# Attention with eight routed experts: sorting the tokens of six half batches by expert, and computing keys and queries half a batch at a time

## The reference

```
latent = (x@Wk + x@Wv) @ W_down_kv;  k = latent@W_up_k;  v = latent@W_up_v;  q = x@Wq
scores = clip(q.k * scale) * exp(-0.0001*|i-j|);  attn = softmax(scores)
x = layernorm(x + (attn@v) @ Wo)
logits = x@w_router; top 2 of 8 experts, softmax of their two logits = weights
moe = sum over the 2 chosen e of weight * (silu(x@fc1[e][:, :128]) * (x@fc1[e][:, 128:])) @ fc2[e]
shared = (silu(x@gate_w) * (x@up_w)) @ down_w          # width 256
x = layernorm(x + moe + shared)
```

## Time and profile before

| | us |
|---|---|
| median of 3 runs | 810.48 (803.38 to 810.81) |
| the profiled execution | 815.1 |
| its span, first to last instruction | 813.1 |
| TensorE, ScalarE, VectorE, GpSimd busy | 763.2, 563.2, 367.1, 222.7 |

### The profile page before, as it was taken

How to read it: one execution, slowest core, us unless ns; L and a number is a source line. 1 busy time by engine, 2 the same in 40 slices (tenths; PEclk the granted TensorE clock), 3 DMA queues, 4 the chain that set the end, 5 groups by cost and what they waited for, 6 DMA issues and landing times. The chain is left out here.

```text
span 813.1 us, 14409 instructions
## 1 busy us (share of the span) xinstructions
PE 763.2 (94%) x4889; PEld 344.9 (42%) x4889; DVE 367.1 (45%) x974; ACT 563.2 (69%) x686; POOL 222.7 (27%) x168
## 2 busy tenths in 40 slices
PE   6736999999999999999999999999999999999996
PEld 4422333333333333333333333334666665665664
DVE  1733233232333233333233333333777777777774
ACT  4635799997999999999999999996222222222221
POOL 1619478392000000000000000000534534534533
PEclk9876699997999999999999999999999999999999
DMA  6489939688323324224233242700000000000000
GB/s 178 160 287 233 318 101 323 233 257 276 86 52 85 70 52 101 54 56 99 52 77 77 52 91 64 174 1 15 1 2 25 27 0 26 26 0 26 13 7 20
DMA packets 27797, 77.17 MB, mean 95 GB/s; under 512 B 2496, under 2 KB 18304, under 8 KB 20608
## 3 DMA queue, kind: packets, MB, share of 16 engines
q1 hardware_dynamic: 24320, 51.74, 25.8%
q0 software_dynamic: 3456, 25.17, 8.5%
HBM read 41.24 MB, written 35.65 MB: 95 GB/s over the span
## 5 line engine op out<-in xcount | busy, mean ns | idle before, releaser
L520 ACT ACTIVATE probs<-ps 128x1024 f32<-128x1024 f32 x480 | 446.8, 1063 | 32.4 <-DVE ps L897 21.9
L661 PE MATMUL ps<-probs,Vring 128*32 128x512 f32 x2048 | 282.4, 624 | 0.7 <-ACT probs L525 0.7
L897 DVE TENSOR_TENSOR ps<-ps,cpk 128x256 f32<-128x256 f32 x256 | 109.9, 432 | 321.4 <-PE ps L646 319.2
L646 PE MATMUL ps<-stacks 32*128 32x512 f32 (+3 forms) x1408 | 221.8, 403 | 17.8 <-DMA stacks<-stack_dram 13.1
L646 PEld LDWEIGHTS ps<-stacks 32*128 32x128 f32 x1408 | 115.9, 189 | 266.1 <-ACT probs L520 222.9
L542 ACT ACTIVATE qT<-ps 128x512 f32<-128x512 f32 x80 | 47.8, 597 | 184.9 <-PE ps L628 184.9
L425 POOL TENSOR_TENSOR small<-small 128x4 f32<-128x4 f32 x8 | 8.2, 1020 | 347.2 <-DVE small L862 347.2
L442 POOL TENSOR_TENSOR kT<-kT 128x512 f32<-128x512 f32 x56 | 71.5, 1276 | 56.9 <-DVE kT L1005 56.1
L753 PEld LDWEIGHTS ps<-stage,kT 128*128 128x128 f32 x512 | 65.0, 191 | 41.2 <-issue 27.5
L753 PE MATMUL ps<-stage,kT 128*128 128x128 f32 x512 | 69.6, 279 | 7.6 <-DVE kT L999 7.5
L999 DVE TENSOR_TENSOR kT<-qT,ps 128x512 f32<-128x512 f32 x80 | 54.3, 683 | 48.3 <-ACT qT L542 47.4
(11 more groups left out here) (115 smaller groups left out, 527.7 us busy)
## 6 DMA issues: line engine op xcount, KB each, us to landing
stacks<-stack_dram SPq DMA_DIRECT2D x64, 512.0 KB, 6.4
stack_dram<-stage POOLq DMA_DIRECT2D x24, 1024.0 KB, 10.6
stack_dram<-stage SPq DMA_DIRECT2D x16, 512.0 KB, 6.0
probs<-in_L_attn_x SPq DMA_DIRECT2D x4, 512.0 KB, 4.8
ptmp<-in_L_attn_x SPq DMA_DIRECT2D x8, 256.0 KB, 3.0
out<-qT SPq DMA_DIRECT2D x8, 256.0 KB, 2.4
rows_sb<-in_decay_rows SPq DMA_DIRECT2D x2, 512.0 KB, 6.6
stage<-in_L_ffn_fc_w SPq DMA_DIRECT2D x1, 1024.0 KB, 8.9
```

Of the source, the lines that this page charges most:

```text
L520: nc.scalar.activation(probs[:, m % 6, :], slot[m % 3], ACT.Exp, scale=SCALE).then_inc(score_slots_free, 1)
L646: last = mm(slot[m % 3][:, h * HALF + lo - q0:h * HALF + hi - q0], sv[rows, u, 1, v, kt * P:(kt + 1) * P], sv[rows, u, 0, v, lo:hi], start ...
L661: last = mm(bank[6][r:r + 32, :], Vring[:, u, kt, h, :], probs[:, (2 * g + qh) % 6, h * HALF:(h + 1) * HALF], start=(kt == 0), stop=(kt == ...
L897: tt(d, d, diag_fix.unsqueeze(1).to_broadcast([P, 2, P]), ALU.mult).then_inc(diag_done, 1)
```

## The change

Nearly every line is new, and the slow path is moved to the end: the fast path always runs, and `flag` is read after it.

- *Preparation* is for half batches 0 and 1 alone. During attention, in the loop over eight half batches c, TensorE does the side work of c+2 (turn x, project q, k, values, norms) and of c-1 (turn a, Wo, turn the normed rows, router) in `beside(c, t)` at fixed slots t of the 32 tiles, through one PSUM bank; VectorE takes each product in `take(c, t)`. GpSimd splits all four parts of half batch c+2 but those of the first two.
- *Attention* goes by four heads and 512 queries: 32 quads with 8 tiles of two exponentials each. The four heads' 32 rows stand in the four row tiles of TensorE. `load_quad` brings 1 MB of keys and 512 KB of queries, two buffers.
- *Routed experts* of half batches 0 to 5 (GROUP = 6): VectorE counts the tokens of each expert and gives each token two rows in a list that is sorted by expert and rounded up to 56 blocks of 128. GpSimd scatters the normed rows there (`send`, 48 indirect DMAs of 128 rows); four blocks are a unit; SP loads a unit's rows and each block's expert weights, whose number it reads into a register; results go to `result_dram`, and GpSimd gathers two results for each token (`fetch`, 48 indirect DMAs). Half batches 6 and 7 are computed densely as before.
- The work after attention is one written list, through a ring of eight PSUM banks.

The diff's core (GpSimd's order in attention, the list of work, the scatter, gather and layer norm):

```
+            def send(k):
+                for s in range(2):
+                    pool.indirect_dma_start(out=sorted_dram, out_offset=bass.IndirectOffsetOnAxis(ap=slots[:, s, k:k + 1], axis=0),
+                                            in_=xn[:, k // CT, tok(k % CT)], in_offset=None,
...
+            def fetch(c):
+                if c >= 2:
+                    pool.wait_ge(combined, c - 1)
+                for s in range(2):
+                    for t in range(CT):
+                        pool.indirect_dma_start(out=gathered[:, c % 2, s, tok(t)], out_offset=None, in_=result_dram,
...
+            for c in range(NCH):
+                d, p = c - 1, c + 2
+                if p < NCH:
+                    pool.wait_ge(side_kept, numbers["q", p])
...
+                    split(0, p, 0)
+                if d >= 0:
+                    ln1_power(d)
+                if p < NCH:
+                    pool.wait_ge(side_kept, numbers["k", p])
+                    squares_of(p)
+                    split(0, p, 1)
+                    split_end()
+                    split(1, p, 0)
+                    split(1, p, 1)
+                    split_end()
+                if d >= 0:
+                    gap_power(d)
+                if c == GROUP:
...
+                    for k in range(SENT_EARLY):
+                        send(k)
+            for k in range(SENT_EARLY, GROUP * CT):
+                send(k)
...
+            for u in range(2):
+                pool.wait_ge(results_stored[u], 16 * UNITS // 2)
+            fetch(0)
+            fetch(1)
+            ln2_power(0)
+            fetch(2)
...
+            def split(n, p, v):
...
+                rest(nc.gpsimd.tensor_tensor(hi, src, tab, ALU.mult))
+                link(nc.gpsimd.tensor_tensor(pool_f[:, v, :], src, tab, ALU.mult))
+                rest(nc.gpsimd.tensor_tensor(lo, pool_f[:, v, :], hi.bitcast(F32), ALU.subtract))
...
+        work = [("shared", 0), ("shared", 1), ("unit", 0), ("unit", 1)]
+        for c in range(2, GROUP):
+            work += [("shared", c), ("unit", 2 * c - 2), ("unit", 2 * c - 1)]
+        for u in range(2 * GROUP - 2, UNITS, 2):
+            work += [("dense", GROUP, u // 2 - GROUP + 1), ("unit", u), ("unit", u + 1)]
+        work += [("dense", GROUP, e) for e in range(UNITS // 2 - GROUP + 1, E)] + [("shared", GROUP)]
+        work += [("dense", LAST, e) for e in range(E)] + [("shared", LAST)]
...
+            def take(c, t):
...
+                if t == 7 and has_d:
+                    add_residual(taken(("wo", d)), d).then_inc(side_kept, 1)
+                    dve.wait_ge(side_kept, numbers["wo", d])
+                    statistics(y_pre[:, :], stats, mv, var, var_ready)
+                if t == 8 and has_p:
+                    keep_values(p, taken(("v", p))).then_inc(side_kept, 1)
+                if t == 8 and has_d:
+                    ln1_rows(d)
+                if t == 10 and has_d:
+                    keep(("x", d), xnT[:, d, :])
...
+            def beside(c, t):
...
+                if t == 9 and has_d:
+                    dst = side(("x", d))
+                    pe.wait_ge(xn_ready, d + 1)
+                    turn(dst, xn[:, d, :]).then_inc(side_ready, 1)
```

More of the change, by code:

```diff
@@ new lines, in values, with norms @@
+            def values(p):
+                dst = side(("v", p))
+                for t in range(CT):
+                    last = mm(dst[:, tok(t)], xT[:, p % 2, tok(t)], wfold[:, 3, :], start=True, stop=True)
+                last.then_inc(side_ready, 1)
+            def norms(p):
+                dst = side(("norm", p))
+                pe.wait_ge(squared, p + 1)
+                for n in range(2):
+                    last = mm(dst[32 * n:32 * n + 32, :], head_sum_h[:, :], squares[:, n, :], start=True, stop=True)
+                last.then_inc(side_ready, 1)
@@ new lines, in _ @@
+            pe.wait_ge(s_experts, 5 * 16)
+            for k in range(len(work) + 1):
+                if k + 1 < len(work) and work[k + 1][0] == "unit":
+                    turn_block(work[k + 1][1])
+                if k < len(work):
+                    for i in range(2 if work[k][0] == "shared" else 1):
+                        up(work[k], i, 0)
+                        up(work[k], i, 1)
+                if k:
+                    down(work[k - 1])
+                if k in LAST_STEPS:
+                    last_step(k)
@@ new lines, in _, with taken @@
+            dve.wait_ge(s_rows, 32)
+            dve.wait_ge(first_kept, 4)
+            split(0, 0)
+            dve.wait_ge(first_kept, 5)
+            split(1, 1)
+            for h in range(2):
+                dve.wait_ge(first_ready, 5 + h)
+                keep_values(h, (bank[SIDE_BANK], bank[1])[h]).then_inc(first_v_kept, 1)
+            count = [0]
+            def taken(name):
+                count[0] += 1
+                assert numbers[name] == count[0], name
+                dve.wait_ge(side_ready, count[0])
+                return bank[SIDE_BANK]
@@ new lines, in _ @@
+            for k in range(len(work) + 1):
+                if k < len(work):
+                    for i in range(2 if work[k][0] == "shared" else 1):
+                        hidden(work[k] + (i,))
+                if k and work[k - 1][0] != "unit":
+                    add_down(work[k - 1])
+                if k in LAST_STEPS:
+                    last_step(k)
+                if k and work[k - 1] == ("shared", GROUP):
+                    dve.wait_ge(ring_by_dve, ring["dn", "shared", GROUP][2])
+                    ln2_statistics(GROUP)
+                if k in COMBINE_AFTER:
+                    combine(COMBINE_AFTER[k])
+                    ln2_statistics(COMBINE_AFTER[k])
```

1820 lines of the change are left out of this document (1074 added, 746 removed).

## The result

The changed kernel took 900.34 us in the median of four runs (897.58 to 902.88), the kernel before 806.93 us (802.6 to 810.81) beside it: a ratio of 1.116, 95% interval 1.108 to 1.124. It is slower, outside the predicted range of 692 to 808 us. In two later batches of runs the same kernel took 901.27 and 897.75 us (ratio 1.114, interval 1.106 to 1.123) and 838.25 and 833.27 us (1.034, interval 1.024 to 1.044). So there are two results, by the batch and its chip, and both are slower and outside the range.

The account below looks back on a forecast made before the run. ScalarE's exponentials were taken to bound attention, TensorE the expert part. 46 + 475.5 + 5 + 5 + 3 + 27.5 + 15 + 98 + 66 = 741, plus 2.0 around the span: 743 us, range 692 to 808.

Parts of the forecast that it names:

- first exponential: Start: preparing only half batches 0 and 1 brings the first exponential to 46 us, against 65.67; bounds 41 and 54.
- port waits and the clock behind them: Half batches 1 to 5: 5.5 us lost each at VectorE's port wait, 27.5; low clock after each 3, 15 us.
- other stalls, half batches 0 to 7: Attention: 5 us for groups overrun by projections, 5 for one low-clock stay, 3 for a late load.
- last exponential to first gather: Experts' first part: dense passes, 14 units, layer norm and routing 88 us, plus 10 of weight waits: 98 us.
- first gather to the end: Experts' second part: 48 gathers at 1.1 us set the pace, then last combination and end: 66 us.
- The 48 scatters hide in attention up to 1.68 us each: End of attention: GpSimd's scatters delay nothing if each takes at most 1.68 us, 81 us from half batch 6.
- Rival (c): Scatters and gathers: indirect DMA dear on GpSimd, gain gone at 2.1 us each, 850 us at 2.5; chance 0.09.
- The side work: Attention: about 9 us of TensorE work per half batch fits 27 us of idle time; overruns cost 5 us in all.
- the late load: First half batch: the third load, queued behind stores and clearing, comes 3 us late (0 to 10).
- The port wait: Half batches 1 to 5: VectorE's four row operations wait for GpSimd's run, then go in one gap; 5.5 us each.
- rival (a): Half batches 1 to 5: each row operation waits anew, 13.3 us plus 5.8 for low clock, 796 us; chance 0.20.
- Rival (b): Half batches 1 to 5: VectorE is served at once and the clock holds, 42.5 us less, 700 us; chance 0.20.

Follow-up runs that it names:

- e13: The changed kernel with no further change, run once more on chip 12, without the stalls: 835.76 us (two runs).
- e4: Against the changed kernel, one added wait: GpSimd begins its squares and splits only after VectorE's normed rows are done; 824.77 us.
- e10: The changed kernel word for word, run again on chip 1, with the stalls: 899.51 us (two runs).
- e18: Against the changed kernel, the 22 scatters of half batch 6 are plain DMAs to result_dram, half batch 7 unchanged; 874.98 us on chip 1.

## Why the prediction was wrong

The sum was 741 us of span. Without the stalls (e13, span 836.5) and with them (the profile after, 901.0) its terms were:

| term | predicted | without stalls | with stalls |
|---|---|---|---|
| first exponential | 46 | 55.7 | 54.8 |
| port waits and the clock behind them | 27.5 + 15 | 27.4 + about 7 | the same |
| other stalls, half batches 0 to 7 | 5 + 5 + 3 | about 59 | about 114 |
| 512 exponentials | 475.5 | 475.6 | 475.6 |
| last exponential to first gather | 98 | 120.3 | 120.5 |
| first gather to the end | 66 | 91.6 | 101.1 |

The span is 160 us above the sum. The stalls make 64.5 us of it, which only one chip has, and the rest, 95.5 us, every chip: without the stalls, too, the kernel would have been slower than before (3.4%) and outside the range (835.76 us). So more than one step failed, and the larger part of the miss isn't the spectacular one. The 7 us for the clock are an estimate: in e13 the intervals in the ten exponentials behind the port waits add up to 13.5 us above the pace, of which 6.8 stand there at full clock in e4 as well.

**The step that failed on the chip with stalls** is "The 48 scatters hide in attention up to 1.68 us each". Their price on GpSimd was well bounded (0.54 to about 3; 1.28 measured), and nobody waits for them; but I asked only what they cost their own queue. What they do to the other engines cost 56 us in attention (e10 against e13, the same program: stalls of 28.5 and 39.6 against 7.3 and 4.9), and the second part, with its 48 gathers, is 8 us longer on that chip too (100.0 against 91.5). Rival (c) had the sign, "the indirect DMA on GpSimd is dear", but put its price into a duration, 2.1 us from which it would decide; by that rule it should not have mattered.

**The side work, 13 us against 59: the step that failed on every chip.** It is "waiting 0.84 us of every 1.86 us for ScalarE to free a score slot: its real need is about 1.0 us". The row that has 0.84 is one of PEld, the loader of weights: it stands idle from 301.43 to 302.26 while the value products run. The matmul rows of the same trace leave no such gap:

```profile
301.27 1.07 PE L661 MATMUL ps<-probs,Vring 128*32 128x512 f32 x8
302.27 0.91 PE L646 MATMUL ps<-stacks 32*128 32x256 f32 x6
303.11 1.07 PE L661 MATMUL ps<-probs,Vring 128*32 128x512 f32 x8
```

The value products take 1.0 us from their start to the next row, and the scores 0.84 at ScalarE's pace. Where TensorE is behind, as in the timeline further down, the scores take 0.44 to 0.49. The need is thus about 1.45 us a group, and some 0.4 of 1.86 are free, half of what I had (an estimate from these rows). "TensorE gets about 9 us ... into 32 x 0.84 = 27 us of idle time" becomes 9 into 13, and it doesn't come spread out. The timeline of half batch 1:

```profile
133.37 1.12 PE L808 MATMUL ps<-xT,Wq_sb 128*128 128x512 f32 x2 [0.36 <-DVE a_tok L1117]
134.43 0.56 PE L774 MATMUL ps<-queries,keys 32*128 32x128 f32 x8
134.92 1.04 PE L787 MATMUL ps<-probs,V 128*9 128x512 f32 x8
135.02 0.76 DVE L1244 TENSOR_TENSOR ps<-ps,cpk 128x256 f32<-128x256 f32 x2 [1.70 <-PE ps L774]
135.69 0.68 DVE L1109 COPY qk<-ps 128x512 f32<-128x512 f32 x1
136.43 0.66 PE L729 MATMUL ps<-cpk,a_tok 128*128 128x128 f32 x4 [0.46 <-DVE qk L1109]
```

From 133.37 to 136.43 it is 3.06 us, where ScalarE needs 1.86 for a group. TensorE's own work makes 2.6 of them: projection, scores and values one after the other, 0.7 more than the pace, where I had 0.2. The other 0.46 are a wait. All side products share one PSUM bank, and a product must wait until VectorE has emptied it, behind its own correction of the diagonal. ScalarE then idles 0.5 to 1.3 us in most such groups, 4 to 6 us ahead of the port wait in each of half batches 1 to 5. This is read from the rows; no run spread the side work or gave it a second bank, so how the 59 us divide between the two isn't shown. The start of half batch 0 and its end (intervals of 3.3 and 3.8 us, the latter the late load that I had forecast) and the first groups of half batches 6 and 7 belong to them too.

**The port wait had the right place and size, by a mechanism that was half wrong, so the size is luck in part.** The rows of half batch 2 (L866 is now L1130), and all 24 of attention:

```profile
220.95 4.88 DVE L1130 TENSOR_SCALAR xn<-y_pre,small 128x128 f32<-128x128 f32 x4
...
226.86 1.94 ACT L684 ACTIVATE probs<-ps 128x1024 f32<-128x1024 f32 x2 [5.32 <-DVE ps L1244]
```

```profile
L1130 DVE TENSOR_SCALAR xn<-y_pre,small x24: 343/1198/1419, 146.9 to 512.6; 128x128 f32<-128x128 f32 x24
```

The intervals were 6.25 to 6.6 us in place of 0.93 in all five half batches, at exponential 21 or 19 as forecast: 27.4 us in e13 against 27.5. From within each on the granted clock was 0.50 (1.2 GHz) for some 7 us, which cost about 7 us in all five, not 15. But I had VectorE wait for the end of GpSimd's run and then have all four served in one gap. The two engines alternate instead: GpSimd's operations follow each other with no gap or 0.08 us (second square to 221.96, then 223.18, 224.41, 225.75), and one L1130 ends some 0.08 us after each of them (222.04, 223.26, 224.49, 225.83). Each waits for one operation of 1.26 us, and 4 x 1.2 happens to be what one long wait would have been. So the rule of the Trainium skill (SBUF — State Buffer, Who interferes with whom), a lock for a whole instruction to whoever issues first, agrees with this trace (a median of 1.198 us for 0.343), each L1130 competing anew; rival (a) had that right and took a whole run of operations as its price, 13.3 us where it is 5.5. Rival (b) is out by the same rows.

In e4, where GpSimd's squares and splits wait for the normed rows, the same operation takes its plain time; what comes after it doesn't. The rows of e4: normed rows, and three steps of VectorE's routing, which take 0.166, 0.182 and 0.190 us in the changed kernel:

```profile
L1132 DVE TENSOR_SCALAR xn<-y_pre,small x24: 330/341/347, 145.7 to 502.3; 128x128 f32<-128x128 f32 x24
L1150 DVE TENSOR_TENSOR small<-small x6: 166/1126/1190, 155.7 to 511.5; 128x4 f32<-128x4 f32 x6
L1156 DVE CAST small<-small x6: 181/1006/1235, 158.1 to 512.3; 128x32 f32<-128x32 uint32 x6
L1159 DVE TENSOR_TENSOR onehot<-cpk,small x12: 179/700/1307, 159.4 to 512.6; 128x32 f32<-128x32 f32 x12
```

The delayed splits now lie beside the routing, which goes with the intervals of 3.2 and 3.1 to 4.0 us at exponentials 29 and 33 of the odd half batches, and with about 9 us won where 34 were at stake. A conflict at a shared port that is moved meets the next user.

**The start, 46 against 55.** I gave the 12 splits of each engine 1.28 us, that of an undisturbed one. Both engines now split at once, and most took 1.5 to 1.76 us (one of each engine, and the load behind them):

```profile
27.69 1.75 DVE L1071 TENSOR_TENSOR osb<-qk,rows_sb 128x512 f32<-128x512 f32 x1
...
27.29 1.59 POOL L524 TENSOR_TENSOR stage<-pool_f,stage 128x512 fp32r<-128x512 f32 x1
...
45.10 0.37 SPq L366 DMA_DIRECT2D keys<-stack_dram  x1
```

The last split ended at 35.9, not 30, the loads were issued at 45.1, not 37.3, and it took another 9.7 us to the first exponential.

**The experts, 164 us against 212.** I set the waits of the first part at 10 us by the time that the weights take. Two loads stand in one queue, with a wait between them and register loads on top; in each of six pairs of units the chain of waits has 3.1 to 4.6 us of the load of rows, and 3.6 to 6.1 of the load of weights once the rows were ahead. The second part has the gathers right in kind, 1.31 us each for the 1.1 that I took; but with the powers between them, and the waits of these for VectorE, they make 69.9 us in e13, not 53, and 21.7 us stand behind the last one, not 13.5.

## What to carry to other kernels

An operation that runs on an idle engine is free only if it also leaves the others alone; for a form that no trace at hand shows, try a run of them beside full work before building on it, and on more than one chip. When a variant that shouldn't matter changes the time by 7%, run the unchanged program beside it before explaining: a control inside the kernel is better still. Side work is to be priced group by group, by the matmul rows (an idle time of the weight loader isn't one of TensorE) and along the ring through its bank and both engines, not by a sum of idle time.

## What the runs showed of the hardware

- An indirect DMA of 128 rows of 512 bytes keeps GpSimd 0.98 us and the next one begins 0.30 us later (scatter, 1.28 in all; gather 1.31); a plain one of as many rows takes 0.53 to 0.54 us.
- On one chip of four (chip 1, in both batches that it ran; the first batch, whose chip isn't listed, looks the same), a run of indirect scatters on GpSimd brings the other engines of the core nearly to a stop from the fifth to the seventh on until it ends, or some 4 us longer: in e18 TensorE is busy 2.2 of 27 us and ScalarE 2.9, and in the profile after SP's register instructions take up to 0.70 us in place of 0.02 to 0.27. On chip 12 the same program shows nothing of it, nor do programs with the same runs of scatters on chips 0 and 5.
- VectorE and GpSimd operations of 128x512 in fp32 with two inputs took 1.27 us on GpSimd alone and mostly 1.5 to 1.76 us on each engine with both at it; the two alternate operation by operation, so that a VectorE operation of 0.34 us that meets a busy GpSimd takes 1.2.
